# A decoder layer with sorted experts: two groups of three batches in place of three groups of two

## The chip, the cores and the metric

One core of a Trainium2 chip runs the whole program. The metric is device time in microseconds; the numbers below are of runs of this kernel on that one core.

## What is computed

For each of 8 batches of 256 tokens with 128 features: latent attention with a learned choice of far keys (top 96 of 256, the 64 nearest always in), a retention over a context, two layer norms, and then an expert layer. Cut to what the change touches, the expert layer is, in words of the reference: router probabilities over 8 experts, the best 2 of each token kept, and

```python
h   = relu(x @ w1[e] + b1[e])        # 128 -> 512, for each expert e
y_e = h @ w2[e] + b2[e]              # 512 -> 128
out = layernorm(x + sum over the token's 2 experts of p[e] * y_e)
```

Every batch's 256 tokens so make 512 pairs of a token and an expert.

## The kernel before

**Order.** `program` (one list, walked by all five engine queues alike) has steps of 20 slots. Step n runs attention of batch n (`stage_b`, slots 0 to 17, one group of 16 query positions each), the projections and key choice of batch n+1 (`stage_a`), retention of batch n-1 (`stage_c`) and the router of batch n-2 (`stage_d`). Each engine executes its queue in this order, so a wait in one piece holds back all that stands after it on that engine. Step 8 (`NB`) has no attention left: there retention and router of batch 7 end, the remaining expert tiles and then the dense experts run.

**Experts, sorted.** Batches 0 to 5 are in groups of two. Once the router of a group's last batch is through (two steps on, slot 2), `tile_list` on VectorE counts how many rows each expert has, finds a row for every pair (about four operations for each batch, L1985 to L1993), and an expert for each tile of 128 rows. On GpSimd, `tile_list` then scatters the tokens into `sorted_tokens` in HBM: four indirect DMAs for each batch (L863), counted by `d_sent`. On SP's queue `fetch` loads the first experts' weights in slots 4 to 6 and, in slot 5, waits for the scatters of the group's last batch and loads four tiles of rows (L638). A group is padded so that the number of tiles is fixed: `most_tiles` gives 15 for two batches (1024 pairs and up to 8 x 127 rows of padding).

**Tiles.** `plan` lays the tiles on slots: in steps 2 to 7 on nine slots of a step (`TILE_SLOTS`), in step 8 on `END_SLOTS`; a group starts at slot 8 of the step of its list. A tile transposes its rows (L919 on `xs`), multiplies with w1 (L1287), takes relu (ScalarE, L1587), multiplies with w2 (L1302), adds b2 (VectorE, L2019) and stores to `expert_rows`. Each loads one expert's weights, 578 KB, into one of 4 buffers. The tiles of the last group that fall in step 8 run in another order with more PSUM banks ("alone").

**Back to tokens.** Two slots after a group's last tile `collect` (GpSimd) gathers four rows sets for each batch (L851), `summed` (GpSimd, L883 to L885) weighs and adds them, `means` and `normed` do the layer norm (VectorE, ScalarE, GpSimd, SP). There are two gather buffers and two sum buffers.

**Experts, dense.** Batches 6 and 7 go through all 8 experts whole: 16 units at the end (L1338, L1352), the first eight on `DENSE_SLOTS` of step 8. The last sorted group's `collect`, `summed`, `means` and `normed` are put between these units by `unit`.

**Other names used below.** L742 to L750 on GpSimd make `kdn`, the keys of batch n+1, which TensorE transposes at slot 7 of step n (L919 on `kdn`); SP copies `gs` to `vstk` once per slot of far attention (L615), and TensorE transposes `vstk` in the next slot.

With three groups of 15, where `(g, k)` is tile k of group g, the plan is: step 3 holds (0,-2) to (0,2), step 4 (0,3) to (0,11), step 5 (0,12) to (0,15) and (1,-2) to (1,2), step 6 (1,3) to (1,11), step 7 (1,12) to (1,15) and (2,-2) to (2,2), step 8 (2,3) to (2,15). In an entry k the w2 product of tile k is made, if 0 <= k < 15; the entries -2 and -1 only start the pipeline and entry 15 only stores.

Of the kernel before, what the change touches and what calls it, by code (L numbers as in the profile page):

```python
# [19 lines left out]
ALU = mybir.AluOpType  # L20
ACT = mybir.ActivationFunctionType
F32 = mybir.dt.float32
BF16 = mybir.dt.bfloat16
# [33 lines left out]

GROUPS = tuple((b, most_tiles(b)) for b in ((0, 1), (2, 3), (4, 5)))
SORTED = sum(len(b) for b, _ in GROUPS)
# [8 lines left out]
WB = B2_AT + DM  # L68
MOST = 16
TILE_SLOTS = (0, 2, 4, 5, 8, 10, 13, 15, 17)  # L70
LIST_SLOT, FIRST_SLOT = 2, 6
FETCH_SLOTS = (4, 5, 6)
SUM_LATE, MEAN_LATE, NORM_LATE = 3, 5, 6
END_SLOTS = (0, 1, 2, 3, 4, 5, 6, 7, 8, 9, 9.5, 10, 11)
DENSE_SLOTS = (11.5, 12, 13, 14, 15, 16, 17, 18, 19)


def plan():
# [9 lines left out]
    for n in range(SORTED):  # L88
        g = GROUP_OF[n]
        if g < LAST:  # L90
            step, s = ends[g]
            s += 2 + 2 * (n - GROUPS[g][0][0])
            for table, late in ((gather, 0), (first, SUM_LATE), (second, MEAN_LATE), (third, NORM_LATE)):
                table[step + (s + late) // NS, (s + late) % NS] = n
# [128 lines left out]
def build(nc, io, out):  # L223
    ctx = ExitStack()
    with ctx:
# [101 lines left out]
        v8, i8, f8 = sb("v8", [128, NB, 2, 8]), sb("i8", [128, 2, 8], U32), sb("f8", [128, 2, 8])  # L327
        hm, hot = sb("hm", [128, 2, 2, 2, NE]), sb("hot", [128, 2, NE], BF16)
        before, ones = sb("before", [128, 128], BF16), sb("ones", [128, 128], BF16)
        taken, place = sb("taken", [128, NE]), sb("place", [128, 2, 2, NE])  # L330
        qq, qs, slot = sb("qq", [128, 4, NE]), sb("qs", [128, 4]), sb("slot", [128, NB, 4], U32)
# [117 lines left out]
        def program(stage_a, stage_b, stage_c, stage_d, tile_list, fetch, tile, collect, summed, means, normed, dense_first, dense_second, dense_end):  # L449
# [1179 lines left out]
        def _(dve):  # L1629
# [270 lines left out]
            def router(i):  # L1900
# [23 lines left out]
                for r in range(2):  # L1924
                    k = od.did(TT(hm[:, i.par, r, :, :], C("expert_no").rearrange("p (o e) -> p o e", o=1).broadcast_to([128, 2, NE]),
                                  f8[:, :, r:r + 1].broadcast_to([128, 2, NE]), ALU.is_equal))
                od.wait(k)
                TT(hot[:, :, :], hm[:, i.par, 0, :, :], hm[:, i.par, 1, :, :], ALU.add).then_inc(r_m.sem, 1)

            oe = Own(dve, own_ve)  # L1930

            def gates(i, k):

                for r in range(2):
                    k = oe.did(TT(hm[:, i.par, r, :, :], C("expert_no").rearrange("p (o e) -> p o e", o=1).broadcast_to([128, 2, NE]),
                                  f8[:, :, r:r + 1].broadcast_to([128, 2, NE]), ALU.is_equal))
                oe.wait(k)
                d = DENSE.index(i.n)
                for t in range(2):
                    k = oe.did(TS(gg[:, d, t, :], hm[:, i.par, 0, t, :], v8[:, i.n, t, 0:1], None, ALU.mult))  # L1940
                oe.wait(k)
                for t in range(2):
                    last = STT(gg[:, d, t, :], hm[:, i.par, 1, t, :], v8[:, i.n, t, 1:2], gg[:, d, t, :], ALU.mult, ALU.add)
                last.then_inc(r_gate.sem, 1)

            def stage_d(s, i):
# [10 lines left out]
                if s == 3 and i.n not in DENSE:  # L1957

                    dve.wait_ge(r_full.sem, r_full.at(i.n, 2))
                    since = C("nothing") if i.n == GROUPS[GROUP_OF[i.n]][0][0] else taken[:, :]  # L1960
                    k = od.did(TT(place[:, p, :, :], bR[:, 16:32].rearrange("p (t e) -> p t e", t=2),
                                  since.rearrange("p (o e) -> p o e", o=1).broadcast_to([128, 2, NE]), ALU.add))
# [5 lines left out]
            def tile_list(g):  # L1968
# [13 lines left out]
                for b in batches:  # L1982
                    os_.batch(-1, b)
                    base = row0[:, :].rearrange("p (o e) -> p o e", o=1).broadcast_to([128, 2, NE])
                    k = os_.did(TT(place[:, b % 2, :, :], place[:, b % 2, :, :], base, ALU.add))  # L1985
                    os_.wait(k)
                    k = os_.did(TT(qq[:, :, :].rearrange("p (r t) e -> p r (t e)", r=2),
                                   hm[:, b % 2, :, :, :].rearrange("p r t e -> p r (t e)"),
                                   place[:, b % 2, :, :].rearrange("p (o t) e -> p o (t e)", o=1).broadcast_to([128, 2, 2 * NE]), ALU.mult))
                    os_.wait(k)  # L1990
# [119 lines left out]
```

## Time and profile before

| | us |
|---|---|
| median of 3 runs | 667.35 |
| lowest, highest | 665.1, 670.21 |
| the profiled execution | 671.91 |
| its span, first to last instruction | 670.1 |

| engine | busy us | share of the span |
|---|---|---|
| TensorE, matmul | 569.7 | 85% |
| VectorE | 433.0 | 65% |
| ScalarE | 407.6 | 61% |
| GpSimd | 265.1 | 40% |

The 16 DMA engines moved 75.84 MB, a mean of 113 GB/s. The mean granted TensorE clock was 0.919. The profiled execution is 4.6 us above the median of the runs, so a sum made on its rows is carried over to the median as a difference.

### The profile page before, as it was taken

Reading aid. Unit: us, or ns where it says so; the run is one execution under the profiler, and the core shown is the slowest. Engines: PE = TensorE matmul, PEld = TensorE weight load, DVE = VectorE, ACT = ScalarE, POOL = GpSimd, SP = SyncE. Lnnn points to the kernel's source line nnn. Section 1 sums busy time; section 2 is a strip of 40 time slices with the busy share of each in tenths; the row PEclk is TensorE's granted clock in tenths of the full one; section 3 lists DMA queues with packets and bytes.
Section 4 is the critical chain, followed back from the end, with each engine's and each line's share of the span. In section 5 each row is a group of like instructions: output and inputs, shape, how many; then the busy total and the mean of one; then the engine's idle time right before and its main releaser. Section 6 shows DMA issues by size and latency. Waiting matters only on the chain.

```text
span 670.1 us, 22002 instructions
## 1 busy us (share of the span) xinstructions
PE 569.7 (85%) x8149; PEld 437.9 (65%) x8149; DVE 433.0 (65%) x1618; ACT 407.6 (61%) x1381; POOL 265.1 (40%) x428
## 2 busy tenths in 40 slices
PE   5378987896898679989997897979995999789996
PEld 4154764574566457866787566757785667678886
DVE  0947647965885797568755894668657676434653
ACT  4446666674776567658774675568765556545352
POOL 1414901931380388016601698317502663104310
PEclk9757797998899789979997799889999899999999
DMA  5030144114013151553344143543353534785551
GB/s 169 2 123 18 22 142 177 22 26 125 13 27 115 31 158 30 172 177 104 105 148 128 49 144 86 180 134 108 108 162 105 160 95 134 221 244 187 177 159 43
DMA packets 58593, 75.84 MB, mean 113 GB/s; under 512 B 14256, under 2 KB 47480, under 8 KB 57336
## 3 DMA queue, kind: packets, MB, share of 16 engines
q1 hardware_dynamic: 56952, 71.30, 35.7%
q0 software_dynamic: 1536, 3.15, 1.6%
q8 instruction: 65, 1.06, 0.7%
q14 instruction: 40, 0.33, 0.2%
HBM read 58.92 MB, written 8.62 MB: 101 GB/s over the span
## 4 chain that ended last, share of the span: by engine, by line
PE 34%; POOL 10%; ACT 8%; issue 7%; DVE 6%; DMA 1%; SPq 0%; DVEq 0%; POOLq 0%; ACTq 0%
PE bW L1352 4%; PE bR L1302 4%; PE bH L1287 3%; PE bG L1075 3%; POOL gb L851 3%; PE bM L919 3%; ACT qV L1555 2%; PE bH L1338 2%; PE bG L1338 2%; ACT ht L1587 2%; PE bS L1094 2%; PE bM L1122 1%; PE bM L1117 1%; POOL sorted_tokens L863 1%; PE bC L1227 1%
## 5 line engine op out<-in xcount | busy, mean ns | idle before, releaser
L1503 ACT ACTIVATE ppn<-pp,rls 128x224 f32<-128x224 f32 (+1 forms) x128 | 58.9, 460 | 33.9 <-DVE rls L1803 32.9
L1821 DVE TENSOR_TENSOR gs<-bG,rank_t 96x512 f32<-96x512 f32 x96 | 65.5, 682 | 17.9 <-PE bG L1075 15.8
L1495 ACT ACTIVATE pp<-pp,nmx 128x224 f32<-128x224 f32 x96 | 46.5, 484 | 30.2 <-DVE nmx L1814 29.3
L809 POOL TENSOR_TENSOR r<-x,cst 128x256 f32<-128x256 f32 x8 | 5.8, 724 | 141.9 <-DVE x L1848 141.9
L1075 PE MATMUL bG<-oh,kspl 128*96 128x512 f32 x160 | 60.2, 459 | 0.0
L1884 DVE TENSOR_TENSOR sm<-bC,cst 128x512 f32<-128x512 f32 x64 | 43.6, 681 | 23.7 <-PE bC L1227 23.7
L1587 ACT ACTIVATE ht<-bH,wt 128x128 f32<-128x128 f32 x156 | 44.4, 371 | 18.0 <-PE bH L1287 18.0
L1513 ACT COPY pts<-bM 128x256 f32<-128x256 f32 x96 | 35.5, 369 | 29.1 <-PE bM L919 28.4
L919 PE MATMUL bM<-cst,ppn 128*128 128x128 f32 (+1 forms) x224 | 49.8, 293 | 3.8 <-ACT ppn L1503 3.4
L1814 DVE CUSTOM_DVE_ANT_0 pp<-bS,cst 128x224 f32<-128x224 f32 x96 | 36.4, 379 | 25.7 <-PE bS L1094 25.5
L1302 PE MATMUL bR<-wt,ht 128*128 128x128 f32 x264 | 40.8, 304 | 9.4 <-DVE taken L1964 9.3
L1302 PEld LDWEIGHTS bR<-wt,ht 128*128 128x128 f32 x264 | 37.8, 215 | 13.5 <-issue 11.0
L1227 PE MATMUL bC<-qV,kS 128*128 128x512 f32 x64 | 33.9, 530 | 14.7 <-DVE sm L1884 8.3
L1122 PE MATMUL bM<-pts,vgs 128*32 128x8 f32 x3072 | 46.3, 182 | 0.0
L1117 PEld LDWEIGHTS bM<-pts,ckw 96*32 96x32 f32 x1024 | 20.8, 111 | 38.4 <-issue 37.5
L1287 PE MATMUL bH<-xt,wt 128*128 128x128 f32 x312 | 44.5, 288 | 1.6 <-DVE xt L2013 1.6
L1094 PE MATMUL bS<-gs,qall 96*32 96x128 f32 x768 | 42.7, 296 | 1.4
L742 POOL TENSOR_TENSOR ktab<-kr,ka 128x64 f32<-128x64 f32 x8 | 2.6, 321 | 103.6 <-ACT ka L1469 80.8
L851 POOL DMA_INDIRECT gb<-expert_rows,slot x24 | 25.0, 1041 | 45.4 <-DMA expert_rows<-ot 38.9
L1287 PEld LDWEIGHTS bH<-xt,wt 128*128 128x128 f32 x312 | 41.2, 203 | 2.5 <-DVE xt L2013 2.0
L1122 PEld LDWEIGHTS bM<-pts,vgs 128*32 128x32 f32 x3072 | 42.3, 117 | 0.0
L1091 PE MATMUL bS<-kd,qall 128*128 128x96 f32 x192 | 38.0, 281 | 4.0 <-DVE nmx L1814 3.8
(294 smaller groups left out, 1604.5 us busy)
## 6 DMA issues: line engine op xcount, KB each, us to landing
wt<-in_experts SPq DMA_DIRECT2D x61, 578.0 KB, 4.1
sidx<-far_slots SPq DMA_DIRECT2D x8, 1536.0 KB, 7.0
vstk<-gs SPq DMA_DIRECT2D x96, 64.0 KB
xs<-sorted_tokens SPq DMA_DIRECT2D x45, 64.0 KB, 3.7
expert_rows<-ot SPq DMA_DIRECT2D x45, 64.0 KB, 3.6
sorted_tokens<-acc SPq DMA_DIRECT2D x9, 256.0 KB, 2.9
cst<-shape_constants SPq DMA_DIRECT2D x1, 1595.5 KB, 6.4
xn<-in_x SPq DMA_DIRECT2D x8, 128.0 KB, 3.2
```

The costliest lines, as they stand in the source:

```text
L851: nc.gpsimd.indirect_dma_start(gb[:, n % NG, 2 * k + t, :], None, ys_dram[g][:, :], bass.IndirectOffsetOnAxis(ap=slot[:, n, 2 * k + t:2 * ...
L919: return MM(dst, src, ident[lo:lo + n, lo:lo + n], is_transpose=True, start=True, stop=True)
L1075: last = MM(w[0:96, :], table, oh[:, pair % 2, kt, SLOTS * (tile % 2):SLOTS * (tile % 2) + SLOTS], start=(n == 0), stop=(n == len(products ...
L1094: last = MM(bS[32 * c:32 * c + 32, o + 96:o + SW], qall[0:96, p, 128 * tile + 32 * c:128 * tile + 32 * c + 32], gs[:, g % 2, 128 * c:128 * ...
L1122: last = MM(bM[32 * j:32 * j + 32, WEIGHED:WEIGHED + 32].rearrange("p (a q) -> p a q", a=2)[:, :, 4 * c:4 * c + 4], vgs[:, 32 * c:32 * c + ...
L1287: last = MM(w[:, 128 * f:128 * f + 128], wt[:, t % NW, 128 * f:128 * f + 128], xt[:, t % 2, :], start=True, stop=True)
L1302: last = MM(w[:, 0:128], ht[:, t % 2, f, :], wt[:, t % NW, W2_AT + 128 * f:W2_AT + 128 * f + 128], start=(f == 0), stop=(f == 3))
L1495: AC(pp[:, s % 2, 0:w], bS[:, 0:w] if s < T0 else pp[:, s % 2, :], ACT.Exp, scale=1.0 if s < T0 else -1.0, bias=nmx[:, s % 2:s % 2 + 1], a ...
L1503: AC(ppn[:, t % 2, 0:w], pp[:, t % 2, 0:w], ACT.Copy, scale=rls[:, t % 2:t % 2 + 1]).then_inc(s_nrm.sem, 1)
L1587: last = AC(ht[:, t % 2, f, :], w[:, 128 * f:128 * f + 128], ACT.Relu, bias=wt[:, t % NW, FF + f:FF + f + 1])
L1821: TT(gs[:, g % 2, :].rearrange("p (t j) -> p t j", j=FAR), bG[0:96, :].rearrange("p (t j) -> p t j", j=FAR), rank_t[:, :].rearrange("p (o ...
L1884: free(TT(sm[:, u % 4, :].rearrange("p (v c) -> p v c", v=4), bC[:, :].rearrange("p (v c) -> p v c", v=4), C("causal").rearrange("p (o c) ...
```

## The change

Groups are now (0, 1, 2) and (3, 4, 5); `most_tiles` gives 19 for three batches, so there are 38 tiles where there were 45. By the plan, step 3 has no tile entry any more; step 4 holds (0,-2) to (0,2), step 5 (0,3) to (0,11), step 6 (0,12) to (0,19) on its first eight slots, step 7 (1,-2) to (1,2), step 8 (1,3) to (1,19). The lists are made in steps 4 and 7 (before in 3, 5 and 7) and have three batches each. The first group's `collect` falls on step 6 slot 17, step 7 slot 1 and step 7 slot 5, each `summed` four slots on, `means` seven, `normed` nine. In step 8 sixteen w2 products of sorted tiles run (before twelve), and the dense units begin at slot 13 (before 11.5). The third batch of the last group is collected in unit 7 and finished in units 10 to 12; the norm of dense batch 6 moves from unit 10 to unit 13. `hm` and `place` get a third buffer.

```diff
-GROUPS = tuple((b, most_tiles(b)) for b in ((0, 1), (2, 3), (4, 5)))
+GROUPS = tuple((b, most_tiles(b)) for b in ((0, 1, 2), (3, 4, 5)))
...
-MOST = 16
+MOST = 20
...
-SUM_LATE, MEAN_LATE, NORM_LATE = 3, 5, 6
-END_SLOTS = (0, 1, 2, 3, 4, 5, 6, 7, 8, 9, 9.5, 10, 11)
-DENSE_SLOTS = (11.5, 12, 13, 14, 15, 16, 17, 18, 19)
+SUM_LATE, MEAN_LATE, NORM_LATE = 4, 7, 9
+END_SLOTS = (0, 1, 2, 3, 4, 5, 6, 7, 8, 9, 9.5, 10, 10.5, 11, 11.5, 12, 12.5)
+DENSE_SLOTS = (13, 13.5, 14, 14.5, 15, 16, 17, 18, 19)
...
-            s += 2 + 2 * (n - GROUPS[g][0][0])
+            s += 2 + 4 * (n - GROUPS[g][0][0])
...
-        hm, hot = sb("hm", [128, 2, 2, 2, NE]), sb("hot", [128, 2, NE], BF16)
+        hm, hot = sb("hm", [128, 3, 2, 2, NE]), sb("hot", [128, 2, NE], BF16)
...
-        taken, place = sb("taken", [128, NE]), sb("place", [128, 2, 2, NE])
+        taken, place = sb("taken", [128, NE]), sb("place", [128, 3, 2, NE])
...
                 if e == 1:
-                    for n in late:
-                        collect(n)
+                    collect(late[0])
+                    collect(late[1])
                 if e == 4:
-                    for n in late:
-                        summed(n)
+                    summed(late[0])
+                    summed(late[1])
...
                 if e == 7:
                     normed(late[0])
                     means(late[1])
+                    collect(late[2])
...
                 if v == NE + 2:
+                    summed(late[2])
+                if v == NE + 3:
+                    means(late[2])
+                if v == NE + 4:
+                    normed(late[2])
+                if v == NE + 5:
                     dense_end(0)
```

## Rows read from the trace of the kernel before

**Rows 1.** Busy time by windows: length, engines PE/PEld/DVE/ACT/POOL (instructions), clock, DMA share, GB/s.
```profile
40.77:100.81 60.04, 52.83 (x790) 35.94 (x788) 35.08 (x128) 35.52 (x126) 22.75 (x40) 0.76 0.20 55
...
161.38:221.67 60.29, 51.40 (x870) 35.36 (x870) 44.66 (x167) 40.17 (x138) 23.72 (x45) 0.92 0.18 50
221.67:288.77 67.10, 56.55 (x923) 41.69 (x923) 48.86 (x188) 44.09 (x154) 33.93 (x53) 0.92 0.37 112
288.77:360.46 71.69, 66.90 (x1023) 53.16 (x1023) 48.79 (x185) 49.57 (x174) 24.55 (x45) 0.95 0.45 133
360.46:438.03 77.57, 66.77 (x972) 51.30 (x972) 53.02 (x209) 46.95 (x166) 49.68 (x71) 0.87 0.38 111
438.03:508.45 70.42, 64.41 (x1015) 50.85 (x1015) 48.88 (x185) 48.62 (x171) 24.57 (x45) 0.98 0.45 133
508.45:571.50 63.05, 54.48 (x932) 42.23 (x932) 43.83 (x161) 38.80 (x143) 31.77 (x38) 0.97 0.41 114
571.50:602.90 31.40, 26.49 (x227) 23.85 (x228) 11.94 (x31) 16.44 (x50) 2.39 (x4) 1.00 0.77 229
```

**Rows 2.** Timeline of GpSimd in step 3: start, length, instruction, idle before in brackets.
```profile
239.34 0.96 POOL L863 DMA_INDIRECT sorted_tokens<-x,slot  x1 [0.30 <-issue]
240.61 0.96 POOL L863 DMA_INDIRECT sorted_tokens<-x,slot  x1 [0.30 <-issue]
...
244.19 0.32 POOL L750 TENSOR_TENSOR kdn<-kg 128x64 f32<-128x64 f32 x1
```

**Rows 3.** Timelines of TensorE and of SP's queue in step 3.
```profile
244.71 0.38 PE L919 MATMUL bW<-cst,kdn 128*128 128x128 f32 x2
...
244.94 1.84 SPq L638 DMA_DIRECT2D xs<-sorted_tokens  x4
246.88 0.56 SPq L615 DMA_DIRECT2D vstk<-gs  x1
```

**Rows 4.** Timeline of VectorE in step 3's list, start of two batches.
```profile
229.45 0.17 DVE L1985 TENSOR_TENSOR place<-place,row 128x16 f32<-128x16 f32 x1
...
230.31 0.18 DVE L1985 TENSOR_TENSOR place<-place,row 128x16 f32<-128x16 f32 x1
```

**Rows 5.** Timeline of GpSimd in step 7.
```profile
516.35 1.12 POOL L863 DMA_INDIRECT sorted_tokens<-x,slot  x1 [5.56 <-DVE slot L1993]
...
525.59 1.79 POOL L863 DMA_INDIRECT sorted_tokens<-x,slot  x1 [0.30 <-issue]
...
541.73 1.07 POOL L883 TENSOR_TENSOR gb<-gb,v 128x512 f32<-128x512 f32 x1
...
544.38 1.05 POOL L883 TENSOR_TENSOR gb<-gb,v 128x512 f32<-128x512 f32 x1
```

**Rows 6.** Timeline of SP's queue in step 7.
```profile
528.08 0.46 SPq L647 DMA_DIRECT2D wt<-in_experts  x1
530.28 2.45 SPq L638 DMA_DIRECT2D xs<-sorted_tokens  x4
532.84 0.55 SPq L615 DMA_DIRECT2D vstk<-gs  x1
```

**Rows 7.** Timeline of VectorE in step 8, the last operation of two tiles.
```profile
584.17 0.29 DVE L2019 TENSOR_TENSOR ot<-bW,wt 128x128 f32<-128x128 f32 x1 [0.60 <-PE bW L1302]
...
586.29 0.29 DVE L2019 TENSOR_TENSOR ot<-bW,wt 128x128 f32<-128x128 f32 x1 [0.60 <-PE bW L1302]
```

**Rows 8.** Busy time by windows, around a GpSimd-caused wait in step 5 (columns as in the first).
```profile
413.00:418.00 5.00, 1.75 (x13) 1.47 (x13) 1.70 (x8) 0.69 (x5) 4.63 (x7) 1.00 0.26 97
418.10:424.90 6.80, 6.68 (x74) 4.87 (x75) 4.85 (x24) 4.99 (x21) 4.55 (x7) 0.50 0.17 41
```

**Rows 9.** Timelines of VectorE and of TensorE at the norm of dense batch 6.
```profile
645.67 0.49 DVE L1829 BATCH_NORM_STATS2 fst<-xr 128x6 f32<-128x128 f32 x2
...
646.38 1.95 PE L1352 MATMUL bW<-wt,qall 128*128 128x128 f32 x16
648.16 1.04 PE L1338 MATMUL bH<-x2T,wt 128*128 128x256 f32 x4
```

More of the change, by code:

```diff
@@ L1924, in router @@
                 for r in range(2):
-                    k = od.did(TT(hm[:, i.par, r, :, :], C("expert_no").rearrange("p (o e) -> p o e", o=1).broadcast_to([128, 2, NE]),
+                    k = od.did(TT(hm[:, i.n % 3, r, :, :], C("expert_no").rearrange("p (o e) -> p o e", o=1).broadcast_to([128, 2, NE]),
                                   f8[:, :, r:r + 1].broadcast_to([128, 2, NE]), ALU.is_equal))
                 od.wait(k)
-                TT(hot[:, :, :], hm[:, i.par, 0, :, :], hm[:, i.par, 1, :, :], ALU.add).then_inc(r_m.sem, 1)
+                TT(hot[:, :, :], hm[:, i.n % 3, 0, :, :], hm[:, i.n % 3, 1, :, :], ALU.add).then_inc(r_m.sem, 1)
             oe = Own(dve, own_ve)
@@ L1934, in gates @@
                 for r in range(2):
-                    k = oe.did(TT(hm[:, i.par, r, :, :], C("expert_no").rearrange("p (o e) -> p o e", o=1).broadcast_to([128, 2, NE]),
+                    k = oe.did(TT(hm[:, i.n % 3, r, :, :], C("expert_no").rearrange("p (o e) -> p o e", o=1).broadcast_to([128, 2, NE]),
                                   f8[:, :, r:r + 1].broadcast_to([128, 2, NE]), ALU.is_equal))
@@ L1939, in gates @@
                 for t in range(2):
-                    k = oe.did(TS(gg[:, d, t, :], hm[:, i.par, 0, t, :], v8[:, i.n, t, 0:1], None, ALU.mult))
+                    k = oe.did(TS(gg[:, d, t, :], hm[:, i.n % 3, 0, t, :], v8[:, i.n, t, 0:1], None, ALU.mult))
                 oe.wait(k)
                 for t in range(2):
-                    last = STT(gg[:, d, t, :], hm[:, i.par, 1, t, :], v8[:, i.n, t, 1:2], gg[:, d, t, :], ALU.mult, ALU.add)
+                    last = STT(gg[:, d, t, :], hm[:, i.n % 3, 1, t, :], v8[:, i.n, t, 1:2], gg[:, d, t, :], ALU.mult, ALU.add)
                 last.then_inc(r_gate.sem, 1)
@@ L1960, in stage_d @@
                     since = C("nothing") if i.n == GROUPS[GROUP_OF[i.n]][0][0] else taken[:, :]
-                    k = od.did(TT(place[:, p, :, :], bR[:, 16:32].rearrange("p (t e) -> p t e", t=2),
+                    k = od.did(TT(place[:, i.n % 3, :, :], bR[:, 16:32].rearrange("p (t e) -> p t e", t=2),
                                   since.rearrange("p (o e) -> p o e", o=1).broadcast_to([128, 2, NE]), ALU.add))
@@ L1984, in tile_list @@
                     base = row0[:, :].rearrange("p (o e) -> p o e", o=1).broadcast_to([128, 2, NE])
-                    k = os_.did(TT(place[:, b % 2, :, :], place[:, b % 2, :, :], base, ALU.add))
+                    k = os_.did(TT(place[:, b % 3, :, :], place[:, b % 3, :, :], base, ALU.add))
                     os_.wait(k)
                     k = os_.did(TT(qq[:, :, :].rearrange("p (r t) e -> p r (t e)", r=2),
-                                   hm[:, b % 2, :, :, :].rearrange("p r t e -> p r (t e)"),
-                                   place[:, b % 2, :, :].rearrange("p (o t) e -> p o (t e)", o=1).broadcast_to([128, 2, 2 * NE]), ALU.mult))
+                                   hm[:, b % 3, :, :, :].rearrange("p r t e -> p r (t e)"),
+                                   place[:, b % 3, :, :].rearrange("p (o t) e -> p o (t e)", o=1).broadcast_to([128, 2, 2 * NE]), ALU.mult))
                     os_.wait(k)
```

## The prediction, made before the change was run

> **What bounds the kernel now.** I read the page first: TensorE is busy 85% of the span and no other engine above 65%, so tiles look like the thing to save. Then I cut the span at the first row maximum of each batch's attention, which stands at the start of a step, and took the busy time by windows [rows 1]. The reader is to see three kinds of step there. Steps 0 and 2 have no expert work and last 60.0 and 60.3 us. Steps 4 and 6 have nine w2 products (nine tiles' worth of work) and last 71.7 and 70.4 us, with TensorE busy 93% and 91%. Steps 3, 5 and 7 hold a list as well. Step 3, with a list and three products, takes 67.1; step 5, with a list, six products and the return of a group, takes 77.6. Step 7 has no projections of a next batch and lasts 63.05 to the end of its tiles; step 8's twelve tiles end 31.4 us later, and the dense units fill the rest. So TensorE bounds the steps with tiles only in part: between tiles, a chain from TensorE over VectorE and ScalarE bounds each slot. Last I went through the timelines of GpSimd and SP's queue around the lists, because the lists get longer.
>
> **Price of a tile inside the steps.** Step 4 less step 2 is 71.69 - 60.29 = 11.4 us for nine products, step 6 less step 2 is 10.1 [rows 1]: 1.1 to 1.3 us a tile.
>
> **Price of a tile in step 8.** Eleven intervals in 31.4 us are 2.85 us a tile, with retention of batch 7 between them [rows 1]. Where little stands between, two tiles' ends are 586.29 - 584.17 = 2.12 us apart [rows 7]. The four added tiles come after most of the retention, which is not added with them. I take 2.2 us, near the close pair, and keep 2.1 and 2.85 for the range. The cover is the DMA share of 0.77 in that stretch [rows 1]: it leaves room, but not much.
>
> **Part by part.**
>
> Step 3 loses its list and its tiles and becomes a step 2: 67.10 -> 60.3, that is -6.8 us.
>
> Step 4 becomes the former step 3 with a third batch in the list. Two prices are added. VectorE's list gets one batch more, 230.31 - 229.45 = 0.86 us [rows 4], and VectorE stands in the chain: +0.9. GpSimd issues four scatters more. One takes 240.61 - 239.34 = 1.27 us start to start [rows 2], so +5.1 us, and what is queued behind it there is `kdn`. It ended at 244.19 + 0.32 = 244.51, and TensorE took it up at 244.71 [rows 2, 3]: slack 0.2 us. TensorE, itself 0.9 later by the list, would then wait 5.1 - 0.2 - 0.9 = 4.0 us. SP's queue waits at the same place: its row loads went out at 244.94, the last scatter's instruction ended at 241.57, and the copy `vstk` stands right behind the loads [rows 2, 3]. Landing took 530.28 - 527.38 = 2.9 us in step 7, where SP visibly waited for it [rows 5, 6], so in step 4 the loads go 4 us late too. Both holds lie side by side: 4.0 us once. New step 4: 67.1 + 0.9 + 4.0 = 72.0 against 71.7, +0.3.
>
> Step 5 becomes the former step 4, or 6: 77.57 -> 71.7 or 70.4, I take 71.5, -6.0 us. The return of a group, whose eight gathers, sums and norms stood here, goes to step 7.
>
> Step 6 has seven products in place of nine, none after slot 13. By the price above 60.3 + 7 x 1.2 = 68.7; I take 68.3, -2.1 us, since the two that go stood at its end.
>
> Step 7 loses the three products of the older group, 3 x 1.1 or somewhat less: -2.5 us. The list gets 0.9 longer. The rest is GpSimd's queue. Before, it was free at 516.35 - 5.56 = 510.8, waited for the list and scattered eight times until 527.4 [rows 5]. Now between these stand the gathers of batch 1 (4 x 1.26 = 5.1) and the sum of batch 0, 544.38 - 541.73 = 2.65 us [rows 5]: the first scatter starts at 510.8 + 7.7 = 518.5 or 2.2 later than before, and twelve end 15.2 later at 533.7. Landed: 536.6, where the loads of rows before went at 530.3. SP would have reached them at 528.08 + 0.46 = 528.5 [rows 6], now 1.6 earlier (-2.5 + 0.9), 526.9, and so is held for 9.7 us instead of 1.7. Behind the loads (2 us) stands `vstk` (532.84 before) [rows 6], and behind that TensorE, then VectorE. `vstk` now goes out at about 538.7, where without the hold it would be about 531.2: 7.5 us, of which SP's hold before had cost about 0.6. I take +6.6. A third batch of norms on VectorE adds 0.7. In sum -2.5 + 0.9 + 6.6 + 0.7 = +5.7 us. There is no `kdn` here, as no next batch is left.
>
> Step 8: four tiles more, 4 x 2.2 = +8.8 us.
>
> Dense units: nothing. The third late batch's gathers go in while GpSimd is idle, its sum is due three units later, and its norm is like the one of dense batch 6, beside which TensorE ran without a gap (646.38 + 1.8 to 648.16, no idle shown) [rows 9]. If that cover were gone, one norm would cost about 2 us.
>
> **The clock.** In step 5, TensorE was busy only 1.75 of 5.00 us while the sums on GpSimd held VectorE, and in the next 6.8 us the granted clock was 0.50, that is 1.2 GHz [rows 8]. Each new hold is likely followed by such a stretch. Bounds: step 0 at a mean clock of 0.76 took 60.04 us, no more than step 2 at 0.92, so nothing [rows 1]; or half of 6.8, 3.4 us. Both new holds lie in slots without tiles, nearer the first: 1 us each, +2.0.
> The Trainium skill, TensorE: Matmul & The Clock Gate, section HAM oscillation, counts the extra time as the throttled time x (1 - 1.2/2.4). By that rule two stretches would cost 6.8 us and the sum would be 4.8 higher; rows 1 do not bear that out for steps bound by a chain.
>
> **Sum.** -6.8 + 0.3 - 6.0 - 2.1 + 5.7 + 8.8 + 2.0 = +1.9 us on 670.1, or 672.0 of span. Its whole time was 671.91, so 673.8; carried to the median, 667.35 + 1.9 = 669.3. I say 669.
>
> **Rivals.**
>
> *The queues hold nothing (faster).* The four added scatters in a list, and those gathers ahead of them, could be hidden. That takes away 4.0 + 6.6 + 2.0 = 12.6 us: 656.7. For it: seven tiles fewer and GpSimd idle 60% of the span. Against it: the slack of 0.2 us at `kdn` and SP's wait already seen at 530.28. It decides where the lists' last scatter lands before SP comes to the loads, which would need scatters at under 0.5 us. Chance 0.2; about half that again (0.1) for only one of the two holds being real, at 661 to 665.
> The Trainium skill, DMA: Bandwidth & Descriptors, section Anatomy of one DMA, says that descriptor generation is small and that many descriptors can be emitted before the cost shows. By that rule this rival would be right; the trace's 1.27 us from one scatter to the next speaks against it.
>
> *The low clock costs its full half (slower).* If both holds are followed by 6.8 us at 1.2 GHz with TensorE bound, and the longer hold in step 7 by a second stretch, the price is 3 x 3.4 = 10.2 in place of 2.0: 677.5. For it: rows 8, with 6.68 of 6.80 us busy. Against: steps 0 and 2. Chance 0.15.
>
> *Step 8's tiles wait for weights (slower).* At 2.85 us each instead of 2.2 they cost 11.4, +2.6; with the late sums of step 7 holding VectorE 2 to 3 us more, 674.5. Chance 0.1.
>
> *Much as forecast:* 0.45. Step 3, 5 and 6 are comparisons of whole steps and could be off together by 2 us.
>
> **How the numbers follow.** About 1% (6.7 us) is what a measurement of this kernel can tell from no change, so faster means below 660.7 and slower above 674.0. The first rival gives 0.2 faster, with 0.02 of its half case; the forecast and the half case stay within, save for 0.04 on the slow side; the second is slower, 0.15, and half of the third. That makes 0.22, 0.54 and 0.24. The range leaves out half of the first rival's part and the upper part of the second: 658 to 678.
>
> **What would show it.** Right: step 3 at about 60 us, step 5 at about 71; in step 4 an idle of about 4 us on TensorE before the `kdn` transposes, with GpSimd named; in step 7 SP's row loads 8 to 10 us after its last weight load, `vstk` behind, and GpSimd without idle from the gathers of batch 1 to the last scatter; the stretches after them at clock 0.5; sixteen tiles' ends of step 8 about 2.1 to 2.5 us apart at the end of the row. Wrong: the last scatter of step 4 landing before SP's loads, step 7 no longer than 63 us, or tile ends of step 8 apart by 3 us.

## The result, and the profile after

The changed kernel took 679.67 us (median of 4 runs, 678.65 to 680.56), the kernel before 666.92 beside it: a ratio of 1.0142, interval 1.0093 to 1.019. That is slower, by 12.75 us where 1.9 had been forecast. The median lies above the bound of 1% (674.0) and 1.7 us above the range; the interval of the ratio begins just under 1%, and the ratio on the 667.35 us from which the forecast was made gives 676.8, inside the range. The profiled execution of after took 680.56 us with a span of 678.8. Lines of after are those of before plus 7 (scatters L863 are now L870).

Windows by step of the kernel after, with the columns of [rows 1]. The first two rows are steps 0 and 2, then steps 3 to 7, the last is step 8 from the end of its first tile to that of its last.

```profile
40.64:100.03 59.39, 51.98 (x789) 35.42 (x788) 35.15 (x127) 35.58 (x126) 22.64 (x40) 0.77 0.21 60
160.63:220.92 60.29, 50.73 (x870) 34.96 (x870) 44.68 (x166) 40.18 (x138) 23.75 (x45) 0.94 0.18 50
220.92:281.00 60.08, 49.79 (x870) 34.49 (x870) 44.32 (x167) 40.20 (x138) 23.55 (x45) 0.94 0.18 50
281.00:353.69 72.69, 59.19 (x923) 43.23 (x923) 50.00 (x193) 44.59 (x154) 37.18 (x57) 0.88 0.35 105
353.69:422.95 69.26, 64.12 (x1023) 50.60 (x1023) 48.73 (x185) 49.61 (x174) 24.57 (x45) 1.00 0.49 145
422.95:491.66 68.71, 61.88 (x971) 48.13 (x971) 47.47 (x179) 45.90 (x159) 26.64 (x44) 0.90 0.29 84
491.66:567.60 75.94, 57.66 (x891) 42.46 (x891) 46.73 (x169) 37.12 (x137) 44.75 (x53) 0.77 0.34 99
567.60:612.00 44.40, 36.75 (x334) 33.56 (x335) 15.36 (x46) 21.33 (x67) 2.38 (x4) 1.00 0.82 240
```

Against [rows 1], in the same cuts:

| | before | after | difference | predicted |
|---|---|---|---|---|
| start of step 3 | 221.67 | 220.92 | -0.75 | 0 |
| step 3 | 67.10 | 60.08 | -7.0 | -6.8 |
| step 4 | 71.69 | 72.69 | +1.0 | +0.3 |
| step 5 | 77.57 | 69.26 | -8.3 | -6.0 |
| step 6 | 70.42 | 68.71 | -1.7 | -2.1 |
| step 7, to a tile's end in step 8 | 63.05 | 75.94 | +12.9 | +5.7 |
| step 8's tiles | 31.40 | 44.40 | +13.0 | +8.8 |
| dense units | 67.2 | 66.8 | -0.4 | 0 |
| clock, counted apart | | | | +2.0 |
| span | 670.1 | 678.8 | +8.7 | +1.9 |

Steps 3 to 6 gave 16.0 us, 1.4 more than forecast. Steps 7 and 8 took 25.9 where 14.5 had been forecast. The medians are 12.75 us apart and the two profiled executions 8.65, because the profiled one of before stands 5 us above its median; the traces cover 8.7, and the other 4 us are in no trace.

In step 7 TensorE's busy time grew by 57.66 - 54.48 = 3.2 us (at a mean clock of 0.77 in place of 0.97) and its idle time by 9.7. Its waits from 492 to 571 us in the kernel after, longest in sum first (engine, line, what it waited for: us in sum, times, the longest):

```profile
PE bM L926 <- DMA vstk<-gs: 5.6, 2, 3.7
PE bS L1095 <- ACT pp L1502: 5.1, 2, 3.5
PE bC L1234 <- DVE sm L1891: 4.3, 1, 4.3
PE bC L926 <- POOL rqn L821: 2.7, 2, 2.5
```

And in the kernel before, from 508 to 571 us, where `rqn` is not among them:

```profile
PE bR L1302 <- DVE taken L1964: 3.3, 1, 3.3
PE bS L1088 <- ACT pp L1495: 1.7, 1, 1.7
PE bC L1227 <- DVE sm L1884: 1.5, 1, 1.5
PE bM L919 <- DMA vstk<-gs: 0.7, 1, 0.7
```

Two of the four waits of after end in GpSimd's queue: `rqn` directly, and `vstk` by way of SP. GpSimd's timeline of after in step 7 (start, length, line and work, idle before it and what ended it):

```profile
487.79 1.02 POOL L858 DMA_INDIRECT gb<-expert_rows,slot  x1 [24.48 <-DMA expert_rows<-ot]
...
495.06 0.72 POOL L821 TENSOR_TENSOR rqn<-r 128x256 f32<-128x256 f32 x1
495.93 1.47 POOL L858 DMA_INDIRECT gb<-expert_rows,slot  x1
...
501.43 1.07 POOL L890 TENSOR_TENSOR gb<-gb,v 128x512 f32<-128x512 f32 x1
...
504.29 1.04 POOL L870 DMA_INDIRECT sorted_tokens<-x,slot  x1 [0.15 <-DVE slot L2000]
...
519.35 0.97 POOL L870 DMA_INDIRECT sorted_tokens<-x,slot  x1 [0.31 <-issue]
520.62 0.98 POOL L858 DMA_INDIRECT gb<-expert_rows,slot  x1 [0.30 <-issue]
...
529.03 1.59 POOL L901 TENSOR_SCALAR acc<-acc,fmv,fln 128x128 f32<-128x128 f32 x2
```

From 495.9 to 530.6 it has no gap longer than 0.31 us: the gathers of batch 1 and the sum of batch 0, twelve scatters, the gathers of batch 2, the sum of batch 1, the norm of batch 0. And it starts late, because its first gather (487.79) stood waiting for the store of the last tile, with the rotation of the query heads (`rqn`) queued behind it. SP's queue over the same stretch:

```profile
515.59 0.45 SPq L654 DMA_DIRECT2D wt<-in_experts  x1
522.12 1.75 SPq L645 DMA_DIRECT2D xs<-sorted_tokens  x4
523.97 0.55 SPq L622 DMA_DIRECT2D vstk<-gs  x1
...
530.65 0.39 SPq L706 DMA_DIRECT2D out<-acc  x1
531.14 7.84 SPq L622 DMA_DIRECT2D vstk<-gs  x4
```

SP is held twice: by the rows, 6.1 us (515.59 + 0.45 to 522.12, forecast 9.7), and then by the store of batch 0's result (L706), which waits until GpSimd's norm at 529.03 has ended. `vstk` stands behind both. Counted from the step's start, `vstk` behind the rows went out at 523.97 - 491.66 = 32.3 us, where the prediction has 538.7 - 508.45 = 30.3: only 2 us of the 7 that step 7 is over its forecast lie ahead of that point, the rest behind it. The chain of the work that ended last (start, us, what) says the same:

```profile
529.83 0.80 POOL acc L901
530.65 0.39 SPq L706
531.14 2.09 DMA vstk<-gs
533.27 0.90 PE bM L926 x3
```

### The profile page after: what moved, and what is told of

It is laid out like the page before. It is cut to its first block, busy times and chain, and to the rows that moved or that the text cites. A ratio compares the mean times of both kernels' runs of the same rounds, so it can differ in the third digit from the quotient of the medians.

```text
span 678.8 us, 21626 instructions
## 1 busy us (share of the span) xinstructions
PE 560.5 (83%) x8030; PEld 424.8 (63%) x8030; DVE 430.7 (63%) x1598; ACT 402.0 (59%) x1353; POOL 265.2 (39%) x428
## 3 DMA queue, kind: packets, MB, share of 16 engines
q1 hardware_dynamic: 53640, 65.80, 32.5%
## 4 chain that ended last, share of the span: by engine, by line
PE 32%; issue 8%; POOL 7%; ACT 7%; DVE 4%; DMA 1%; SPq 0%; DVEq 0%; POOLq 0%; ACTq 0%
PE bW L1359 4%; POOL sorted_tokens L870 3%; PE bH L1294 3%; PE bG L1082 3%; PE bR L1309 3%; PE bM L926 3%; PE bH L1345 2%; ACT qV L1562 2%; PE bG L1345 2%; PE bS L1101 2%; PE bR L1217 1%; PE bM L1129 1%; ACT ht L1594 1%; PE bM L1124 1%; POOL gb L858 1%
## 5 line engine op out<-in xcount | busy, mean ns | idle before, releaser
L1510 ACT ACTIVATE ppn<-pp,rls 128x224 f32<-128x224 f32 (+1 forms) x128 | 58.9, 461 | 32.3 <-DVE rls L1810 31.2
L1082 PE MATMUL bG<-oh,kspl 128*96 128x512 f32 x160 | 60.4, 461 | 0.0
L1891 DVE TENSOR_TENSOR sm<-bC,cst 128x512 f32<-128x512 f32 x64 | 43.6, 682 | 25.4 <-PE bC L1234 25.2
L1520 ACT COPY pts<-bM 128x256 f32<-128x256 f32 x96 | 35.5, 370 | 35.3 <-PE bM L926 34.6
L858 POOL DMA_INDIRECT gb<-expert_rows,slot x24 | 24.9, 1036 | 79.1 <-DMA expert_rows<-ot 72.7
L1821 DVE CUSTOM_DVE_ANT_0 pp<-bS,cst 128x224 f32<-128x224 f32 x96 | 36.4, 379 | 29.6 <-PE bS L1101 29.4
L1101 PE MATMUL bS<-gs,qall 96*32 96x128 f32 x768 | 43.0, 298 | 1.5
L1594 ACT ACTIVATE ht<-bH,wt 128x128 f32<-128x128 f32 x120 | 34.3, 372 | 13.2 <-PE bH L1294 13.2
L1562 ACT ACTIVATE qV<-bC,cst 128x512 fp32r<-128x512 f32 x64 | 38.8, 697 | 3.2 <-PE bC L926 3.2
L1124 PE MATMUL bM<-pts,ckw 96*32 96x32 f32 x1024 | 39.7, 233 | 0.7 <-ACT ots L1529 0.6
L1490 ACT COPY qall<-bW 128x512 f32<-128x512 f32 x32 | 35.5, 1121 | 7.1 <-PE bW L926 7.1
L926 PE MATMUL bM<-cst,vstk 128*128 128x128 f32 x96 | 32.8, 342 | 5.6 <-DMA vstk<-gs 5.6
```

What stands on the lines that cost most here:

```text
L926: return MM(dst, src, ident[lo:lo + n, lo:lo + n], is_transpose=True, start=True, stop=True)
L1082: last = MM(w[0:96, :], table, oh[:, pair % 2, kt, SLOTS * (tile % 2):SLOTS * (tile % 2) + SLOTS], start=(n == 0), stop=(n == len(products ...
L1101: last = MM(bS[32 * c:32 * c + 32, o + 96:o + SW], qall[0:96, p, 128 * tile + 32 * c:128 * tile + 32 * c + 32], gs[:, g % 2, 128 * c:128 * ...
L1124: last = MM(bM[32 * j:32 * j + 32, WEIGHED:WEIGHED + 32], near, pts[0:96, 0:128].rearrange("p (q a b) -> p b a q", a=2, b=4)[:, j, :, :], ...
L1510: AC(ppn[:, t % 2, 0:w], pp[:, t % 2, 0:w], ACT.Copy, scale=rls[:, t % 2:t % 2 + 1]).then_inc(s_nrm.sem, 1)
L1562: last = AC(qV[:, :, v, :], bC[:, :].rearrange("p (g c) -> p g c", g=4), ACT.Copy, scale=C("variant")[:, v:v + 1])
```

## The experiments

Theory: step 7 is long because GpSimd's queue is full from the first gather to the first norm, and TensorE comes to wait for it through `rqn`, the rows, the stores and VectorE's means. Rivals: the tiles themselves are dear wherever they lie; the low clock after the holds costs the time. The twelve runs went in four comparisons, each with runs of the kernel before on its chip. A slot's length below is the interval between two row maxima of one batch's attention. "Slots 0 to 8" runs from the first maximum to the ninth, eight intervals. "To the tile's end" is the cut of the table above; the last column covers the last sixteen tiles (twelve in before), of which four lie in step 7 itself in the last two rows. The expectation of late_return names 79.9 us for step 7 of after: that cut ends one tile later, 75.9 is the figure in the cut used here.

The first column comes from all runs of a kernel, the other three from one profiled execution each, and executions differ. light_weights is the kernel after up to the last tiles of step 8, and its steps 4 to 7 took 73.3, 70.5, 65.7 and 77.6 us where after has 72.7, 69.3, 68.7 and 75.9. A difference of 2 or 3 us in one step's length is therefore no finding by itself; a wait that appears or goes is.

| run | ratio to before, interval | slots 0 to 8 of step 7 | step 7 to the tile's end | tiles of step 8 |
|---|---|---|---|---|
| before | | 25.7 | 63.1 | 31.4 |
| after | 1.0142, 1.0093 to 1.0190 | 32.5 | 75.9 | 44.4 |
| late_return | 1.0193, 1.0120 to 1.0266 | 27.8 | 79.5 | 47.1 |
| store_late | 1.0094, 1.0058 to 1.0129 | 35.4 | 76.0 | 44.1 |
| eight_scatters | 1.0033, 0.9993 to 1.0073 | 34.3 | 73.6 | 43.8 |
| tiles_in_7 | 1.0117, 1.0048 to 1.0186 | 27.6 | 78.1 | 48.1 |
| rows_late | 1.0178, 1.0092 to 1.0264 | 34.3 | 78.4 | 43.5 |
| rows_and_keys | 1.0147, 1.0068 to 1.0226 | 34.7 | 77.5 | 43.4 |
| filler | 1.0159, 1.0075 to 1.0243 | 38.6 | 77.0 | 43.8 |
| light_weights | 1.0167, 1.0079 to 1.0254 | 35.3 | 77.6 | 41.6 |
| return_in_idle | 1.0036, 1.0001 to 1.0071 | 40.3 | 80.8 | 45.2 |
| combined | 1.0026, 0.9991 to 1.0061 | 39.7 | 80.9 | 43.6 |
| combined_more | 0.9993, 0.9954 to 1.0031 | 40.2 | 75.4 | 48.2 |
| combined_again | 1.0105, 1.0065 to 1.0144 | 29.4 | 69.0 | 48.6 |

**late_return: the first group's return at the end of step 7.**

```diff
-SUM_LATE, MEAN_LATE, NORM_LATE = 4, 7, 9
+SUM_LATE, MEAN_LATE, NORM_LATE = 3, 5, 6
+RETURN_SLOTS = (7, 9, 13)
...
-            step, s = ends[g]
-            s += 2 + 4 * (n - GROUPS[g][0][0])
+            step, s = NB - 1, RETURN_SLOTS[n - GROUPS[g][0][0]]
```

> The changed kernel with the return of the first group moved back: gathers of batches 0, 1, 2 at slots 7, 9 and 13 of step 7 (the sums three, the means five, the norms six slots on), all behind the list's scatters. The tiles and the lists stay. In the changed kernel step 7, to the first tile's end of step 8, took 79.9 us where the kernel before took 63.05. Theory A (GpSimd's queue: the gathers and the sum ahead of the scatters, and the stores and means of the return that SP and VectorE wait for between them, hold the step): the scatters start 7 to 8 us earlier, step 7 takes 67 to 70 us, the whole is 10 to 13 us shorter than the changed kernel, about 668. Theory B (the low clock, which comes from a step 7 without tiles and projections in its first slots): the clock stays at 1.2 GHz to about 27 us into the step, step 7 takes 74 us or more, the whole is at most 5 us shorter.

Slots 0 to 8 fell from 32.5 to 27.8 us, and all of it came back: slot 15 to the tile's end took 19.6 us in place of 13.4, since the third batch's sum and norm now lay there, and the next ten tiles 33.2 in place of 29.8. The total did not fall, where both theories had expected it to. It looks as if the return costs VectorE and GpSimd their time wherever it stands; this run alone does not show more than that moving it gains nothing.

**store_late: the stores of the returned batches later in SP's queue.**

```diff
+STORE_AT = {(step, s + (4, 3, 2)[n % 3]): n for (step, s), n in NORM_AT.items()}
...
+                    if stores and (step, s) in STORE_AT:
+                        stores[0](STORE_AT[step, s])
```

> The changed kernel with one thing moved: on SP's queue, the store of a returned batch of the first group to the output is not issued at the slot of its norm but 4, 3 and 2 slots later, so that the copies to vstk do not stand behind a wait for GpSimd's norm. Theory A: the waits of TensorE for vstk behind that store (531.14 after 530.65) go, slots 8 and 10 of step 7 are 2 to 3 us shorter each, together 3 to 5 us of 680. The hold before the row loads (522.12) stays. Theory B (the clock alone): within 1 us of the changed kernel.

TensorE's wait for `vstk` fell from 5.6 us to 0.9, slots 8 to 15 took 27.3 us in place of 30.0, and of the single edits with the whole computation this one came out lowest in the first two comparisons, 3.1 us below the changed kernel by the medians (the intervals of the two ratios overlap). But the step's sum stayed, 76.0, because slots 0 to 8 were 2.9 us longer in this profile, where `rqn` held TensorE for 4.8 us. So SP's store is one real hold, which I had not counted. About 3 us is what lifting it alone gives by the medians and by slots 8 to 15; the total does not show it clear of noise.

**eight_scatters: the third batch's four scatters left out of each list.** Its rows are then not in the sorted table.

```diff
-                    sp.wait_ge(d_sent.sem, d_sent.at(GROUPS[g][0][-1], 64))
+                    sp.wait_ge(d_sent.sem, 128 * (g + 1))
...
+                    if n == GROUPS[g][0][-1]:
+                        continue
```

> The changed kernel, but the third batch of each group is not scattered, so its rows are missing from the tiles: eight scatters in a list in place of twelve; all else is issued as it is. Theory A: in step 4 the 7.6 us of slot 6 go back to 3.3 or so (kdn is there 5 us earlier) and in step 7 the row loads go out 5 us earlier; together 7 to 10 us off the changed kernel's 680. Rival (the scatters are hidden, and the holds come from the list's work on VectorE): 1 us or less.

The total fell to 671.97 us, 1.0033 of before: the largest gain of a single edit, for 2 x 4 scatters that take 10.2 us of GpSimd. Step 4 lost 3.2 us (69.5 in place of 72.7), 3.0 of them in slot 6, close to the 4.0 forecast for its hold; step 7 lost 2.4, most clearly in slot 8 (3.7 us in place of 7.5). SP's rows went out at 515.74, 2.45 us after the weights' issue ended, in place of 6.1:

```profile
512.85 0.44 SPq L654 DMA_DIRECT2D wt<-in_experts  x1
515.74 2.29 SPq L645 DMA_DIRECT2D xs<-sorted_tokens  x4
```

**tiles_in_7: late_return, and the last four entries of the first group, with three w2 products, moved from step 6 into step 7.**

```diff
-            here = next(p for p in free if p >= (batches[-1] + 2, FIRST_SLOT))
+            here = next(p for p in free if p >= (batches[-1] + 2, FIRST_SLOT) and (g == LAST or p < (NB - 2, 6) or p >= (NB - 1, 0)))
```

> As late_return, but group 0 leaves slots 8 to 17 of step 6 free and has its last four entries on slots 0, 2, 4 and 5 of step 7, as the last entries of a group lay before. Theory A alone: step 6 is 3 to 5 us shorter than in late_return and step 7 2 to 3 us longer, so about 1 us less than late_return. With theory B the clock of step 7's first 27 us rises from 0.5 to near 1.0 and step 7 is shorter than in late_return: 4 to 8 us less in all. In either case below the kernel before: 660 to 667.

Step 6 fell from 65.6 us in late_return to 63.5, step 7 went from 79.5 to 78.1. The mean granted clock was 0.80, 0.83 and 1.00 in the three windows of slots 0 to 8 (0.63 over them in late_return), and these slots took 27.6 us against 27.8: three products more and a higher clock, and the same time. The total was 677.99 us against 683.49, with overlapping intervals, and far above the 660 to 667 expected. The same row bears on the forecast: three products more, at a higher clock, made the first slots of step 7 no longer. TensorE waited for `pp` 1.1 us in this run and 5.0 in late_return.

**rows_late: the rows loaded two slots later, the group's first tiles in slots 10 and 11.**

```diff
-FETCH_SLOTS = (4, 5, 6)
+FETCH_SLOTS = (4, 5, 6, 7)
+LISTED_SLOTS = (0, 2, 4, 5, 10, 11, 13, 15, 17)
...
-                if k == 1:
+                if k == 3:
                     sp.wait_ge(d_sent.sem, d_sent.at(GROUPS[g][0][-1], 64))
```

> The changed kernel with the wait for the scatters and the four row loads behind it moved on SP's queue from slot 5 to slot 7 of the list's step, and the group's first two entries from slots 8 and 10 to 10 and 11. GpSimd's queue stays. Theory A (two holds side by side, GpSimd's keys in step 4 and SP's row loads in both steps): step 4 keeps its 7.6 us slot, since kdn still comes late; in step 7 slot 8 falls from 7.5 to about 4 us. In all 3 to 5 us less than the changed kernel. Rival (SP's hold is not what costs): step 7's slot 8 stays at 7 us.

No gain. SP was then held by batch 0's store alone, from 525.6 to 536.38, and TensorE waited for `vstk` 5.1 us:

```profile
525.19 0.45 SPq L655 DMA_DIRECT2D wt<-in_experts  x1
536.38 0.41 SPq L707 DMA_DIRECT2D out<-acc  x1
...
537.53 1.98 SPq L646 DMA_DIRECT2D xs<-sorted_tokens  x4
```

The row hold that the prediction put on the path at 6.6 us is there in the trace of after, but it lies beside the hold at the store, which ends later. Taking it away alone gains nothing.

**rows_and_keys: rows_late, and the third batch's scatters behind the key rotation.**

```diff
             def fetch(g, k):
-                pass
+                if k == 0:
+                    scatter(g, GROUPS[g][0][-1:])
```

> As rows_late, and on GpSimd's queue the third batch's four scatters go from the list (slot 2) to the end of slot 4, behind the keys of the next batch (kdn), before its queries. Theory A: now step 4's slot of 7.6 us falls to about 3.3, another 3 to 4 us off rows_late; some of it may come back at the queries, which have 4 us of slack for 5.1 us of scatters. Rival (step 4's hold is SP's row loads alone): rows_late already shows the gain and this adds nothing.

Step 4 fell from 73.1 us (rows_late) to 71.1, its slot 6 from 7.6 to 5.3, where 3.3 had been expected: about half of the `kdn` hold went. Step 7 has no next batch, and stayed at 77.5.

**filler: 64 small products on TensorE in slots 0 to 7 of step 7.** They only keep it busy; their results are not used.

```diff
+                    if i.last and s < 8:
+                        for m in range(8):
+                            f = 128 * (m % 4)
+                            MM(bH[:, f:f + 128], ident, ident, start=True, stop=True)
```

> The changed kernel with eight added matmuls of 128x128 by 128 in each of the first eight slots of step 7, into a bank that nobody reads then: TensorE is busier where the changed kernel's clock was at 1.2 GHz, and nothing else differs. Rival B (the low clock costs time in step 7): the granted clock in the first 27 us of step 7 rises to near 1.0 and slots 0 to 8, 32.5 us in the changed kernel, become 28 us or less. Theory A (a chain of waits bounds these slots, the clock follows from it): the clock may rise, slots 0 to 8 take 32 to 35 us as before, the whole stays within 2 us or gets longer by 1 to 3.

The clock of 503.3 to 510 and of 515 to 526 us was 1.00, where after had 0.50 from 500 to 519.2, and step 7 took 77.0 us. Neither expectation had what came: slots 0 to 8 took 38.6 us, 6 more than in after, and slots 8 to 15 took 25.0, 5 less, with a wait for `vstk` of 2.0 us in place of 5.6. The filler is work too, as the products of tiles_in_7 are, so neither run gives the clock's price by itself. Neither shows a gain in the total from the higher clock.

**light_weights: the last tiles of step 8 load half of their weights.** The second half is left as it was, so these tiles' rows are not the reference's.

```diff
+                cols = FF + FF // 128 if g == LAST and k >= 12 else WB
```

> The changed kernel, but from tile 12 on the last group's tiles load only w1 and b1 of their expert (half of the 578 KB), so w2 and b2 are those of an older tile. Theory C (the last tiles of step 8 wait for their weights, the DMA engines being 0.89 busy there): the last five intervals, 14.5 us in the changed kernel, fall to 11 to 12 us. Rival (retention's last pieces and the chain between engines set the pace): 14 us or more.

The last five intervals between tiles' ends took 11.7 us in place of 14.6, 2.3 each in place of 2.9. This is the term of step 8, taken apart: 2.3 us a tile without the wait for weights (the 2.2 of the forecast), 0.6 of waiting. The total (1.0167, two runs) did not show those 2.9 us, which is no more than executions of this kernel differ by.

**return_in_idle: gathers, sums, means and norms of the first group in slots of their own.**

```diff
+            for table, slots in ((gather, (1, 5, 9)), (first, (4, 8, 12)), (second, (8, 10, 13)), (third, (9, 11, 14))):
+                table[NB - 1, slots[n]] = n
```

> The changed kernel with one edit: the tables that place the first group's return. Gathers of batches 0, 1, 2 at slots 1, 5, 9 of step 7 (was: 18 of step 6, 2 and 6 of step 7), sums at 4, 8, 12, means at 8, 10, 13, norms at 9, 11, 14. So nothing waits ahead of the rotation of query heads (rqn) on GpSimd, and no sum of GpSimd lies beside VectorE's casts of the token list (the cast L2000 at 500.94 took 1.59 us in the changed kernel, 0.17 in late_return). Theory (GpSimd's queue sets step 7: rqn behind the first gather about 2.5 us, the list about 2.2 us beside the sum, then the row hold): slots 0 to 2 of step 7 take about 11 us (14.3 in the changed kernel), the row hold stays, total 4 to 6 us below the changed kernel. Rival (the return costs its GpSimd time wherever it lies, as late_return showed when it was put at the end of step 7): slots 0 to 2 get shorter and slots 9 to 15 longer by the same, total within 2 us of the changed kernel or above.

**combined: with it the later rows, the third scatters behind the keys, and the later stores.**

> The changed kernel with every partial remedy together: the return's tables of return_in_idle, the loads of three tiles' rows two slots later with the group's first tiles in slots 10 and 11, the third batch's scatters behind the other two at the end of their slot, and the stores of the finished batches on SP at slots 10, 13 and 16 in place of right behind their norms. Theory (three holds side by side at GpSimd's queue: rows, SP's stores that wait for a norm, the mean of a batch; each edit alone leaves the other two standing, which is why store_late took back 3 us and rows_late nothing): step 7 up to the first tile's end in step 8 takes about 66 us (76.0 in the changed kernel), total about 668, 11 below. Rival (step 7 is bound by its sum of work, and the holds only show where its idle time lies): step 7 takes 73 us or more, total 674 or more.

**combined_more: combined, with nine entries of the last group in step 7 and step 8 laid out as before.**

```diff
+FULL_SLOTS = (0, 2, 4, 5, 10, 11, 12, 13, 14, 15, 16, 17, 18)
...
+END_SLOTS = (0, 1, 2, 3, 4, 5, 6, 7, 8, 9, 9.5, 10, 11)
+DENSE_SLOTS = (11.5, 12, 13, 14, 15, 16, 17, 18, 19)
```

> combined with nine entries of the last group in step 7 (slots 10 to 18) in place of five, and step 8 laid out as in the kernel before (13 expert slots, dense products from slot 11.5 on). Tests the term of step 8: there the four extra tiles took 12.6 us with the tail (14.5 us for the last five intervals, 2.9 each, and 30 for the first ten), because step 8 has one transfer load of weights after another (DMA busy 0.83 in it). Theory: under attention a tile costs about 1.9 us, so the four cost 4 to 8 us in step 7 and step 8 gives 12 back: total 4 to 8 below combined, about 663, at or below the kernel before. Rival (tiles cost the same wherever they lie; tiles_in_7 moved three of them and gained nothing): within 2 us of combined.

These three were run side by side, on a chip where the kernel before took 687.75 us (25 runs) and so did not stand as elsewhere. Slots 0 to 2 did as expected (10.3 us in return_in_idle against 14.3), but slot 4 of step 7 took 10.8 to 10.9 us in all three, against 3.3. In it TensorE, VectorE and ScalarE hardly ran for about 7 us. The window of that stretch in combined_more, and one at about the same place in combined_again, the same kernel in another comparison and on another chip (the column order is that of [rows 1]):

```profile
509.20:516.40 7.20, 0.02 (x1) 0.00 (x1) 0.36 (x1) 0.46 (x3) 5.95 (x8) 0.50 0.26 66
```

```profile
506.00:513.00 7.00, 7.00 (x90) 4.47 (x92) 4.36 (x11) 3.18 (x15) 5.47 (x6) 0.50 0.63 184
```

The ratios of this comparison can't be put beside those of the others, and its expectations against after and before were neither met nor refuted by it. Within it, combined_more came out 2.8 us below combined by the medians, with overlapping intervals: under the 4 to 8 that were expected of the tiles' places, and not clearly more than the 2 of the rival.

**combined_again: combined_more once more, on another chip.**

> The kernel of combined_more, unchanged. On the chip of that run the kernel before took 687.75 us at the median, against 667 to 670 in the other comparisons, and all three profiled runs there show one stretch in slot 4 of step 7 (combined_more: 509.2, 7.2 us) in which TensorE, VectorE and ScalarE ran nothing while SP's eleven register instructions between the load of the expert's number and the weights' transfer took 6.2 to 7.3 us (1.9 in the changed kernel). Theory (that stall and the longer tail, 70.5 us against 66.8, belong to that chip): on a chip where the kernel before takes 667 to 670, the stretch is gone, step 7 takes about 68 us to the first tile's end of step 8 and the ratio to the kernel before comes to about 0.995 or less. Rival (the stall comes with the order of the instructions, the return's gathers right ahead of the scatters): the stretch is there again in slot 4 and the ratio stays at 0.9993 or above.

Here the kernel before took 669.75 us. The stretch was gone, so the order of the instructions alone does not bring it. The same tile ended 69.0 us into step 7, near the 68 of the theory, but that flatters it, as this tile now lies in the step itself. Up to slot 15 the step took 67.1 us (62.5 in after), with the tiles in it, and the rest of the program 119.6 (124.6): what step 8 gave, step 7 took. The ratio is 1.0105, not 0.995. TensorE's waits of step 7 show that the old holds had gone (`vstk` is not among them, `rqn` is at 0.7) and which came in their place:

```profile
PE bR L1228 <- DVE xt L2035: 6.8, 1, 6.8
PE bS L1110 <- ACT pp L1517: 5.0, 2, 3.5
```

And its chain of the work that ended last, in slot 10:

```profile
531.34 0.94 POOL gb L869
532.33 1.59 POOL acc L916 x2
533.95 0.50 DVE fst L1851 x2
535.38 0.60 DVE gs L1843
```

The norm of batch 0 (L916) stands behind the gathers of batch 2 on GpSimd, VectorE's statistics for batch 1 wait for it (5.6 us idle), and the copy `xt` stands behind them. The hold moved from SP to VectorE. From the start of step 7 to the end, after took 187.1 us and combined_again 186.7. No version here is faster than the kernel before clear of noise.

## Why the prediction was right or wrong

The forecast was 1.9 us slower and the change measured 12.75. The result lies at the upper end of the range only because the range was 20 us wide. Two terms were too low, steps 7 and 8.

**Steps 3, 5 and 6: right.** Comparing whole steps of the trace gave -14.9 and the profiled execution -17.0. That step 6 came within 0.4 us of its forecast is in part luck, as its length is 65.7 to 68.7 us from one execution to another.

**Step 4: right in mechanism and size.** TensorE's waits there name the `kdn` hold, forecast at 4.0 us:

```profile
PE bW L926 <- POOL kdn L757: 3.5, 1, 3.5
```

Leaving the scatters out gave 3.2 us back in eight_scatters, and the step came out at 72.7 against 72.0.

**Step 7: the step that failed, +5.7 against +12.9.** The chain of the forecast (gathers and sum, twelve scatters, rows, `vstk`) is there, and the row hold was even shorter than forecast, 6.1 us for 9.7, since SP itself came to the rows later. The step that failed is the sum -2.5 + 0.9 + 6.6 + 0.7: it takes the row hold for the whole of what waits behind GpSimd's queue. First, `normed` has a part on SP, the store that waits for GpSimd's norm; I had counted the norms on VectorE alone, at 0.7. store_late prices it at about 3 us. Second, the first gather waits on GpSimd for a tile's store, with `rqn` behind it: 2.7 us here, 3.8 to 4.8 in the variants that leave the gather there. Third, VectorE's list ran beside the sum of GpSimd and took 2.2 us longer (last section). Fourth, these holds lie side by side, so that rows_late took one away without gain; the means on VectorE were next in combined_again. Fifth, the -2.5 us for three products less may not have been there to gain: tiles_in_7 put three into the first slots of step 7, and these took no longer, though at a higher clock. How much each contributes to the 7.2 us is not settled, since single removals don't add up. That GpSimd's time matters, and not only the places in the order, rests on eight_scatters, whose median was 7.7 us lower, the most of all, while every change of the order left the total within 4 us or so of after. Of those 7.7 us, the profiled execution has 2.4 in step 7, so for the 7.2 the cause is argued from the waits and not shown by a run.

**Step 8: a term mis-sized, +8.8 against +13.0.** The 2.2 us were read from two ends 2.12 apart [rows 7]; the mean of [rows 1], 2.85, was there and would have given 11.4. The first ten intervals took 29.8 us, as in the kernel before (29.9). Before has one more, of 1.5 us, and after has five, of 14.6 us in sum, 2.9 each. This was the rival with the wait for weights, given a chance of 0.1. The last tiles' weights landed in 5.4 us (4.3 in the kernel before), and light_weights shows that 0.6 us a tile, 2.9 us in all, is this wait. The other 1.3 us of the 4.2 missed stay open.

**The clock: whether it has a price of its own stays open.** After has 37.5 us of low clock from 481.7 on, far more than forecast, but filler and tiles_in_7, with a higher clock there, showed no clear gain for it, and both added work with the clock. What the low level can cost at most in step 7 can be estimated. TensorE was busy at the clock of 0.50 for 17.2 us from 491.66 to 519.2 and for 6.4 us from 532.9 to 539.7, and in part of that without a pause:

```profile
510.00:519.20 9.20, 9.20 (x109) 5.78 (x112) 6.41 (x23) 4.74 (x19) 7.21 (x7) 0.50 0.51 155
```

The products of L1101 took 422 ns there and 285 from 540 to 560 at a clock of 1.00, those of L1082 on `kspl` 687 and 432, so about 1.5 times as long. By an estimate from these rows, 8 of the 23.7 us are the low clock's. TensorE's busy time in step 7 grew by 3.2 us although three products had gone. How much of the 8 us lay on the path is not known, since behind it TensorE waited for `vstk` in any case. The rule of the Trainium skill (TensorE: Matmul & The Clock Gate, section HAM oscillation), half of the low time, would make 19 us of the stretch of 37.5; TensorE was busy in it for 6.1 + 17.2 = 23.3 us, of which the same estimate gives 8 to the low clock.

**The rivals.** Queues that hold nothing: refuted by `kdn` and `vstk`. Low clock: the nearest by its time (677.5), but what the runs name is another mechanism. Weights: right for the price of a tile. The cost of the holds and that of the tiles were both taken near their lower ends, which left the range's upper end about where the result came out.

**Dense units: right**, at -0.4 for nothing. The 1.8 us read there from [rows 9] is 1.95 in the row; nothing hangs on it.

## What to carry to other kernels

When work is moved behind a queue that is already full, list every instruction of every other engine that waits for that queue, its parts on the DMA queue too; holds side by side can hide one another, so removing one may show nothing, and what told here was to shorten the queue's own work. For the price of one more unit of a pipeline the mean of its intervals was the better guess here, 2.85 for a measured 2.9, than its closest pair, 2.12. Work that moves to where the weights are streamed can cost more there than it gave where it left: here the steps that lost tiles and a list gave 16 us, and four tiles moved to the end took 13 of them back.

## What the runs showed of the hardware

**A VectorE instruction was stretched until GpSimd's ended.** The list of after, on VectorE:

```profile
500.94 1.59 DVE L2000 CAST slot<-qs 128x4 uint32<-128x4 f32 x1
...
502.77 0.60 DVE L1994 TENSOR_TENSOR qq<-hm,place 128x32 f32<-128x32 f32 x1
...
503.63 0.53 DVE L2000 CAST slot<-qs 128x4 uint32<-128x4 f32 x1
```

The first cast ended at 502.53, GpSimd's product (501.43 + 1.07) at 502.50. In every run with the sum beside the list the two casts took 1.58 or 1.59 and 0.52 or 0.53 us, in late_return and combined_again, where gathers or scatters of GpSimd ran beside them but no sum, 0.17 to 0.20. The Trainium skill, SBUF — State Buffer, section Who interferes with whom, says that casts of VectorE can take a port pair that GpSimd shares, that VectorE's operations with two inputs in SBUF contend with GpSimd's reads, and that whoever comes second blocks for the whole instruction. This trace agrees on the blocking: the second and third of the slow operations began after GpSimd's and ended 0.02 to 0.04 us behind it. The first cast began 0.49 us before the product's recorded start and was held all the same; why is not shown.

**An indirect DMA of 128 rows takes mostly 1.27 us of GpSimd from one start to the next, and four left out of each list gave 7.7 us in the whole.** The Trainium skill, DMA: Bandwidth & Descriptors, section Anatomy of one DMA, calls descriptor generation small, which the prediction weighed. How much of the 1.27 us it is no run shows; but the cost of many such transfers showed here, with 24 of them from 487.8 to 526.3.

**In one comparison the kernel before ran 2.7% slower** (687.75 us against 669.75), and all three profiles from it have a stretch in step 7 in which SP's eleven register instructions ahead of a weight load took 6.2 to 7.3 us (1.9 at that place in the changed kernel) while three engines stood. The comparison ran on the chip numbered 15, and so did the first one, in which the kernel before took 670.02 us, so it is not shown that the chip makes the difference. What caused the stretches stays open.
